# First attention of a four-layer kernel: GpSimd's second addition of unit u waits until VectorE has scaled the outputs of unit u-2

## The reference, cut to what matters

```
cp = leaky_relu(einsum('btd,cd->btc', representations, Wc) + bc)
q, k, v = split(cp)                      # 16 heads, widths 8, 8, 64
scores = einsum('bqhd,bkhd->bhqk', q, k) / sqrt(8)
attn = softmax(scores, axis=-1)
out = einsum('bhqk,bkhd->bqhd', attn, v).reshape(B, T, 1024)
proj = leaky_relu(einsum('btv,dv->btd', out, Wo) + bo)
return representations + proj
```

## Time and profile before

| | us |
|---|---|
| median of 3 runs | 1082.43 |
| lowest, highest | 1081.42, 1084.85 |
| the profiled execution | 1076.89 |
| its span, first to last instruction | 1075.1 |
| busy in the span: PE, PEld | 927.4 (86%), 478.3 (44%) |
| DVE | 819.0 (76%) |
| ACT | 547.3 (51%) |
| POOL | 648.8 (60%) |

### The profile page before, as it was taken

One profiled execution on the slowest core, in us unless ns is written; L12 is line 12 of the kernel. 1 busy time (PEld: TensorE's weight loads), 2 busy tenths in 40 slices (PEclk: granted clock), 3 DMA queues, 4 the chain that ended last, 5 costly groups with the idle time before them and its releaser, 6 DMA issues.

```text
span 1075.1 us, 20145 instructions
## 1 busy us (share of the span) xinstructions
PE 927.4 (86%) x7298; PEld 478.3 (44%) x7298; DVE 819.0 (76%) x1295; ACT 547.3 (51%) x927; POOL 648.8 (60%) x560
## 2 busy tenths in 40 slices
PE   5799997889888988988988989599987676689997
PEld 3347552222222222322322222498976332358785
DVE  5864768988988898898898841785489999995513
ACT  2475446556556655655655676244345223246363
POOL 5560505877786666868576998105448887873312
PEclk9899998999999999999999999799999898699999
DMA  9353523111110101111000111657751110044562
GB/s 320 119 186 109 154 62 122 25 39 49 36 45 22 53 18 33 46 29 59 29 22 25 41 35 31 208 166 217 250 187 45 59 33 23 20 148 132 152 188 70
DMA packets 91725, 96.98 MB, mean 90 GB/s; under 512 B 22892, under 2 KB 67948, under 8 KB 91372
## 3 DMA queue, kind: packets, MB, share of 16 engines
q1 hardware_dynamic: 86508, 85.20, 25.9%
q0 software_dynamic: 5120, 10.50, 3.4%
HBM read 70.43 MB, written 24.77 MB: 89 GB/s over the span
## 4 chain that ended last, share of the span: by engine, by line
PE 61%; DVE 21%; issue 7%; POOL 7%; ACT 1%; DMA 1%; SPq 0%; ACTq 0%; DVEq 0%; POOLq 0%
PE ps L228 58%; DVE small L247 5%; DVE on_sb L234 5%; PE ps L231 3%; POOL ar L234 3%; DVE ar L234 2%; POOL psum_sb L234 2%; DVE ar L247 2%; DVE osb L247 1%; DVE acc_sb L234 1%; DVE ps L234 1%; DMA psum_sb<-in_L_bv 1%; DVE psum_sb L234 1%; POOL xsort L288 0%; POOL acc_sb L293 0%
## 5 line engine op out<-in xcount | busy, mean ns | idle before, releaser
L228 PE MATMUL ps<-ar 64*64 64x512 bf16 (+4 forms) x5312 | 542.7, 448 | 36.5 <-DVE ar L234 11.4
L228 PEld LDWEIGHTS ps<-ar 64*64 64x64 bf16 (+2 forms) x5312 | 270.8, 138 | 288.4 <-issue 101.6
L271 ACT ACTIVATE ar<-ps 128x1024 f32<-128x1024 f32 (+2 forms) x336 | 303.9, 908 | 178.9 <-PE ps L228 172.2
L247 DVE TENSOR_REDUCE small<-ps 128x2 f32<-128x1024 f32 (+2 forms) x276 | 306.4, 1137 | 45.7 <-PE ps L228 44.5
L234 POOL TENSOR_TENSOR psum_sb<-psum_sb,ar 128x1024 f32<-128x1024 f32 x96 | 232.0, 2417 | 37.1 <-ACT ar L271 28.1
L234 POOL TENSOR_TENSOR ar<-ar 128x512 f32<-128x512 f32 (+1 forms) x80 | 106.4, 1334 | 35.0 <-DVE ar L247 17.1
L234 POOL TENSOR_TENSOR psum_sb<-ar 128x1024 f32<-128x1024 f32 x32 | 75.9, 2372 | 58.9 <-ACT ar L271 55.7
L293 POOL DMA_INDIRECT gT<-ysort,rt x48 | 46.1, 960 | 98.5 <-issue 97.3
L234 DVE TENSOR_TENSOR ar<-ps,ar 128x256 f32<-128x256 f32 (+4 forms) x56 | 56.4, 1011 | 51.1 <-PE ps L228 43.5
L234 DVE TENSOR_TENSOR on_sb<-osb,rec_sb 128x512 f32<-128x512 f32 x32 | 75.2, 2350 | 0.6 <-DMA rec_sb<-lscr 0.6
L268 ACT COPY ar<-ps 128x256 f32<-128x256 f32 (+1 forms) x84 | 30.6, 383 | 87.5 <-PE ps L228 55.6
(11 more groups left out here) (158 smaller groups left out, 1039.2 us busy)
## 6 DMA issues: line engine op xcount, KB each, us to landing
ar<-in_L_up SPq DMA_DIRECT2D x48, 384.0 KB, 4.1
ar<-in_L_b SPq DMA_DIRECT2D x32, 322.0 KB, 3.8
rec_sb<-lscr SPq DMA_DIRECT2D x64, 128.0 KB, 3.0
scr<-ar SPq DMA_DIRECT2D x48, 128.0 KB, 2.0
ar<-xsort SPq DMA_DIRECT2D x40, 128.0 KB, 2.8
ysort<-ar SPq DMA_DIRECT2D x40, 128.0 KB, 3.7
ar<-scr SPq DMA_DIRECT2D x32, 112.0 KB
xsort<-xs SPq DMA_DIRECT2D x12, 256.0 KB, 6.8
```

Source lines behind the costliest of these rows:

```text
L228: return self.e.matmul(o, l, r, start=start, stop=stop) if self.e else Nothing()
L247: return self.e.tensor_reduce(o, a, AX.X, op, negate=True) if negate else self.e.tensor_reduce(o, a, AX.X, op)
L271: return self.e.activation(o, a, fn, **kw) if self.e else Nothing()
```

## The change

Two lines are added to POOL's `attention`. Ahead of the second addition of unit u (k == 2, for u of 2 and more), POOL waits for ("scaled", u - 2), the event that DVE's multiplication of unit u-2 raises. Nothing else is changed.

```diff
--- before.py
+++ after.py
@@ -2058,6 +2058,8 @@
                         pool.wait_ge(*at("sum", u - 2))
                     pool.tt(a_, Ps[:, (i - 1) % NP, :], Ps[:, i % NP, :], ALU.add).then_inc(*up(("sums", u, 1)))
                 elif 2 <= k <= 4:
+                    if k == 2 and u >= 2:
+                        pool.wait_ge(*at("scaled", u - 2))
                     pool.wait_ge(*at("exp", i))
                     pool.wait_ge(*at("sums", u, k - 1))
                     pool.tt(a_, a_, Ps[:, i % NP, :], ALU.add).then_inc(*up(("sums", u, k)))
```

## The result

The changed kernel takes 1046.95 us (median of 4, 1045.01 to 1048.00) where the kernel before takes 1082.66: a ratio of 0.9666, with a 95% interval of 0.9643 to 0.9689. The profiled execution took 1047.98 us.

A forecast was written before the change was run, and what follows sets the result against it. PE was taken as busiest, idling behind DVE's multiplication, which waits for POOL's addition. Terms 30.4 + 1.4 + (1.2 - 0.7 + 0.85) - 1.85 = 31.3 us, off 1082.43, gave 1051.1 us; range 1044 to 1066.

The forecast's parts named there:

- Place and cause: First attention: DVE's multiplication stands still behind POOL's second addition in 24 units; reordering cuts it from 2.81 to 0.68 us.
- Step 2: PE's projection in each unit: of DVE's 2.13 us gain, 1.6 us lies on the path.
- rival A: PE's gap modelled too small: the whole 2.13 us comes back in 24 units, 1034 us; chance 0.07.
- Steps 3 and 4: POOL's 0.85 us delay a unit is covered, 2.4 or 1.8 us left; late first additions make multiplications about 1.2 us.
- interval 19: One unit with the normalisation's four operations on POOL between units: a gain of 1.4 us.
- Step 5: Layer 1 routing, three units: DVE stalls 1.7 and 0.6 us on POOL's small tiles; gains 1.2, -0.7 and 0.85 us.
- Step 6: End of the loop, where POOL works without a pause: its delay is a loss, -1.85 us in all.
- step of subtracting the saving unchanged: Whole kernel: the saving lies where the granted clock is 1.00, so 31.3 us comes unchanged off the 1082.43 us median.
- B: POOL becomes the bound in some twelve units with gathers, normalisation and routing; 15 us lost, 1067 us; chance 0.15.
- D: The wait is already covered, or PE's gain is given back by ACT or a bank: 1082 us; chance 0.04.
- C: Late first additions meet every multiplication, DVE and POOL serialise: +25 us over 30 units, about 1108 us; chance 0.05.

The follow-up runs named there:

- e2_one_input: Kernel before, no wait, with DVE's multiplication replaced by a copy of osb alone (one SBUF input, softmax division left out): 1043.07 us, ratio 0.9652.
- e6_null_wait: Kernel before plus the same wait in the same place, but on the multiplication of unit u-3, so it never holds POOL: 1083.89 us, ratio 1.0017.
- e3_half_multiplication: Changed kernel with the multiplication on half the columns, the other half of the outputs not scaled: 1047.97 us, ratio 0.9692.
- e10_two_waits_out: Changed kernel without the wait in units 16 and 22: 1129.79 us, one execution, on another chip where the kernel before takes 1162.17 us.
- e8_wait_to_unit_25: Changed kernel with the wait in units 2 to 25 only, left out from unit 26 on: 1048.13 us, ratio 0.9676.
- e11_changed_beside: Changed kernel without further edit, run on the same chip as the candidate for direct comparison: 1045.92 us, ratio 0.9665.
- e5_before_again: Kernel before, no edit, traced a second time: one execution, 1083.05 us.
- e7_late_wait: Changed kernel with POOL's second addition held longer, until PE has made the projection of unit u-2: 1096.94 us, ratio 1.0126.
- the candidate: Changed kernel with the wait in units 2 to 17 only; from unit 18 DVE multiplies ahead of its step's reduction: 1045.29 us (0.9666), 1128.05 us on another chip.

## Why the prediction was right

**Place and cause.** Right: in 24 units DVE stood behind POOL's addition (e2_one_input), and the order of the two instructions was the gain, not the instruction added (e6_null_wait).

**Step 2, 1.6 us on the path.** Right to 0.03 us, in all of the intervals 1 to 14, 16, 17 and 20, and for the reason given: the weight load's idle time falls to 0.81, and e3_half_multiplication shows that a still shorter multiplication gives nothing. The Trainium skill's warning on matmul busy time (Perfetto Trace Analysis, Identifying the Most-Contended Engine) would have led to rival A here; the weight loads were busy 4.27 of 13.75 us in a unit that can't go faster.

**Steps 3 and 4, POOL's delay and the late first addition.** The cover was right (1.95 us left at PE's sum in one parity, for 1.8 forecast, and 2.3 for 2.4 in the other), and so was the late first addition. It made the multiplication 0.94 to 0.96 us in four units, for the 1.2 forecast, and cost nothing. The 1.4 us of interval 19 were too much by 0.45, for another reason: the gap to close was smaller there.

**Step 5, routing.** Wrong in its size and in its place. DVE's waits for small tiles after the change:

```profile
529.81 0.22 DVE L247 TENSOR_REDUCE rt<-small 128x8 f32<-128x64 f32 x1 [1.22 <-POOL small L234]
...
535.85 0.22 DVE L247 TENSOR_REDUCE small<-small 128x8 f32<-128x64 f32 x1 [0.48 <-POOL small L234]
```

They are 1.22 and 0.48 us for the forecast 1.7 and 0.6, and some of it fell in time that DVE had to spare, so 1.1 us were lost and not 2.3 (0.3 of it without POOL's delay too, by e2_one_input). The first small tile of POOL took 0.74 us before (554.92 to 555.66, behind a multiplication that ended at 555.51) and 0.29 after: POOL had waited for DVE there as DVE had for POOL. What the prediction didn't look for was the first tile of the routing, one unit pair earlier, which POOL hands to ACT. POOL, then ACT, then PE of the kernel after:

```profile
497.46 4.86 POOL L234 TENSOR_TENSOR psum_sb<-psum_sb,ar 128x1024 f32<-128x1024 f32 x2
502.28 0.29 POOL L234 TENSOR_TENSOR small<-small 128x64 f32<-128x64 f32 x1
```

```profile
502.61 0.26 ACT L271 ACTIVATE small<-small 128x64 f32<-128x64 f32 x1 [2.21 <-POOL small L234]
```

```profile
503.83 2.56 PE L228 MATMUL ps<-ar 64*64 64x512 bf16 x28 [1.89 <-ACT ar L271]
```

The additions end at 502.32, the tile follows, ACT's exponential of it waits 2.21 us in ACT's order ahead of the loop's own exponential, and PE is idle for 1.89. That is interval 21, 2.05 us short of the full gain: 0.85 by POOL's delay, 1.2 by the pace (e10_two_waits_out and e2_one_input). In sum the three intervals gave 1.76 us for the 1.35 forecast, so the total came out nearer than its parts.

**Two more, not foreseen.** Interval 15, first the timelines of POOL and of DVE before, then of all engines after:

```profile
423.73 7.61 POOL L234 TENSOR_TENSOR psum_sb<-psum_sb,ar 128x1024 f32<-128x1024 f32 x3 [1.09 <-ACT ar L271]
```

```profile
432.12 0.68 DVE L242 SCALAR_TENSOR_TENSOR acc_sb<-acc_sb 128x512 f32<-128x512 f32 x1
```

```profile
401.99 0.68 DVE L234 TENSOR_TENSOR on_sb<-osb,rec_sb 128x512 f32<-128x512 f32 x1
...
402.75 7.37 POOL L234 TENSOR_TENSOR psum_sb<-psum_sb,ar 128x1024 f32<-128x1024 f32 x3 [1.94 <-DVE on_sb L234]
...
404.36 0.30 PEld L228 LDWEIGHTS ps<-on_sb,wA 128*128 128x128 f32 x2 [0.81 <-DVE small L247]
...
408.67 2.00 DVE L242 SCALAR_TENSOR_TENSOR acc_sb<-acc_sb 128x512 f32<-128x512 f32 x1
...
411.86 0.60 PEld L228 LDWEIGHTS ps<-ar 64*64 64x64 bf16 x16 [1.90 <-DVE small L247]
411.86 1.49 PE L228 MATMUL ps<-ar 64*64 64x512 bf16 x16 [1.02 <-DVE small L247]
```

The multiplication is short (0.68) and the weight load waits 0.81. Before, the last addition ended at 423.73 + 7.61 = 431.34, 0.78 us ahead of DVE's leaky ReLU of the attention's output (acc_sb<-acc_sb, two SBUF inputs, 128 x 512). Now it ends at 402.75 + 7.37 = 410.12, and the leaky ReLU starts at 408.67 and ends at 410.67: 2.00 us for 0.68. The collision was moved to the next instruction of the same kind, and PE was idle for 1.02 us. And in interval 18 the chain of waits goes through POOL:

```profile
447.77 2.35 POOL psum_sb L234
450.13 1.23 POOL acc_sb L234
...
451.49 0.64 PE ps L231 x4
```

POOL adds the end of layer 0 behind its additions, and PE's transposes wait for it: 0.87 us. The rows for both were in the trace of before; the prediction asked who waits for the additions, but for the small work behind them only in routing, and not where DVE's other two-input instructions stand.

**Step 6, the end of the loop.** Right in mechanism: the first multiplication there meets the late first addition.

```profile
570.93 3.44 DVE L234 TENSOR_TENSOR on_sb<-osb,rec_sb 128x512 f32<-128x512 f32 x1
...
571.44 2.37 POOL L234 TENSOR_TENSOR psum_sb<-ar 128x1024 f32<-128x1024 f32 x1
...
574.45 2.34 POOL L234 TENSOR_TENSOR psum_sb<-psum_sb,ar 128x1024 f32<-128x1024 f32 x1 [0.64 <-DVE on_sb L234]
575.55 0.30 PEld L228 LDWEIGHTS ps<-on_sb,wA 128*128 128x128 f32 x2 [3.07 <-DVE small L247]
```

It takes 3.44 us, the second addition follows 0.08 us behind it, and the projection's weight load waits 3.07 us: interval 25 is -2.21. The size was taken too large. The forecast gave interval 24 nothing, but it gained about 1 us even without the clock. Net, the intervals 24 to 29 come to -0.34 us for the forecast -1.85, with the clock in both. The windows of interval 26, before and then after (columns as in the earlier trace rows):

```profile
606.54:621.41 14.87, 14.18 (x151) 4.43 (x147) 12.71 (x14) 10.75 (x17) 13.61 (x9) 1.00 0.14 39
```

```profile
575.56:591.38 15.82, 15.55 (x147) 4.94 (x147) 12.37 (x14) 10.38 (x16) 13.80 (x9) 0.89 0.12 36
```

The -0.96 of interval 26 is the clock: PE's own work grew by 1.37 us at a granted 0.89, while the old gap of 0.42 us was closed. The kernel before had its fall in interval 24, where PE was busy 16.09 us at 0.92; in e2_one_input, which has none there, it was busy 14.45. Without both falls the six intervals come to about -0.6, which is an estimate from these four figures. By e8_wait_to_unit_25 beside e11_changed_beside it is -1.0 to -1.6.

**The sum.** 31.3 was forecast, and the loop gave 30.4 in the first trace and 31.5 in the second. It is right partly by luck, because errors cancel. Against the first trace the sum was too high by 0.7 us in interval 0, 1.3 in 15, 0.8 in 18 and 0.45 in 19, and too low by 0.5 in the full units (0.03 each), 0.4 in routing and 1.5 at the end of the loop.

The timed runs gave 4.4 us more than the sum, which the prediction's step of subtracting the saving unchanged left out. The granted clock of each run accounts for it by its size, as bookkeeping and not as a cause that was shown: over 31 runs of before the span times (1 - clock) is 49.6 us on average, over 13 of the changed kernel 45.2; span times clock is 1030.1 and 999.2, 30.9 us apart. The trace the prediction used was of an execution at 0.960, above the mean of 0.954. That the lost falls of the clock lie in the loop was seen in one trace only (e5_before_again); where they lie in the timed runs stays open, and so does whether the change is what makes them fewer. By the same product the two traced executions of the kernel before lost 43 and 51 us to the clock, and the three of the changed kernel 48, 44 and 52, so the traces don't show the difference.

Of the rivals, A is refuted, B and D didn't occur, and C's mechanism exists but needs a longer wait (e7_late_wait).

## What to carry to other kernels

Look for an instruction on VectorE with two SBUF inputs that takes several times its usual duration and whose end is a fixed time behind the end of a GpSimd instruction (here 0.54 to 0.56 us); where it is on the path, let it go first, and see to it that GpSimd starts behind it. Before delaying an in-order engine, list everything behind the delayed instruction up to the next point where that engine rests, with whoever waits for each, small tiles too, and every other two-input instruction that the delayed one can now meet: the large additions were covered here, and what stood behind and beside them cost 0.8 to 0.9 us in each of four units. A gap that is closed is worth what the waiting engine can use, not what the blocking one wins; the idle time of the next weight load where nothing stalls shows that limit.

## What the runs showed of the hardware that was not expected

- The exclusion works both ways. A small tile of POOL took 0.74 us behind a long multiplication and 0.29 without one.
- The granted clock can fall to 1.2 GHz for 3.4 us in the middle of a loop in which PE is idle 1.6 us in every 15.7, in some executions and not in others; the two such falls cost 1.6 and 1.7 us.
- One chip ran the kernel before in 1162.17 us where the others took 1081 to 1083. It wasn't traced there, but the candidate was, there and elsewhere: its loop took 464.05 and 463.05 us, it began at 212 us of the span for 168, and what is behind it took 450.4 us for 411.1. Span times (1 - granted clock) is 86 us there and 47 elsewhere, 39 of the 84 us between the two spans; the rest stays open.
- A wait for what is long over cost POOL 0.05 us, and each of DVE's long multiplications became 0.06 us longer by it, in step with the addition.
